# Six local-attention layers: probabilities times tokens instead of times values, Wv and Wo multiplied by head, the FFN's shift made by transfers, and new instruction orders

## The reference, cut to what matters

```python
def shift_tokens(t):                       # the second half of the features comes from the token before
    a, s = jnp.split(t, 2, -1)
    s = jnp.pad(s, ((0, 0), (1, 0), (0, 0)))[:, :-1]
    return jnp.concatenate([a, s], -1)

def attn_layer(x, Wqkv, qs, ksc, Wo):
    q, k, v = heads(jnp.split(x @ Wqkv, 3, -1))
    q, k = l2norm(q) * qs, l2norm(k) * ksc
    ...                                    # q and k are rotated by tables of cosines and sines
    sim = einsum('bhwie,bhwje->bhwij', q, look(k)) * 8; attn = softmax(masked sim)
    out = einsum('bhwij,bhwje->bhwie', attn, look(v))
    return concat_heads(out) @ Wo

def ffn_layer(x, g, bln, W1, b1, W2, b2):
    xn = layernorm(x) * g + bln
    a, gate = jnp.split(xn @ W1 + b1, 2, -1)
    return a * gelu(gate) @ W2 + b2

x = x + relative_attention(layernorm(x))
y = layernorm(x)
for i in range(6):
    y = attn_layer(shift_tokens(y), ...) + y
    y = ffn_layer(shift_tokens(y), ...) + y
return x + y
```

## Time and profile before

| | us |
|---|---|
| median of 3 runs | 2132.15 (2129.59 to 2133.04) |
| the profiled execution | 2129.15 |
| its span | 2127.4 |
| PE busy | 2025.2 (95%) |
| PEld busy | 1357.7 (64%) |
| DVE busy | 1498.2 (70%) |
| ACT busy | 1285.3 (60%) |
| POOL busy | 1521.0 (71%) |
| share of PE in the chain that ended last | 72% |

### The profile page before, as it was taken

How to read it: one execution, slowest core, us unless ns; L and a number is a source line. 1 busy time by engine, 2 the same in 40 slices (tenths; PEclk the granted TensorE clock), 3 DMA queues, 4 the chain that set the end, 5 groups by cost and what they waited for, 6 DMA issues and landing times.

```text
span 2127.4 us, 84221 instructions
## 1 busy us (share of the span) xinstructions
PE 2025.2 (95%) x35763; PEld 1357.7 (64%) x35763; DVE 1498.2 (70%) x2267; ACT 1285.3 (60%) x1844; POOL 1521.0 (71%) x2315
## 2 busy tenths in 40 slices
PE   6899998979999999999999999999999999999997
PEld 2555555545666667766676666766676666766665
DVE  3445454458877788778777788777787788777873
ACT  4676767535655666566655566566665666566653
POOL 4344444468888788777887788778887788877880
PEclk9999999989999999999999999999999999999998
DMA  6999999922224222242232322224222242222221
GB/s 201 331 347 354 340 352 351 328 73 59 65 67 115 63 66 70 62 114 62 63 73 63 111 68 66 63 64 112 67 72 64 61 118 62 67 63 63 66 70 41
DMA packets 121588, 261.51 MB, mean 123 GB/s; under 512 B 29140, under 2 KB 36224, under 8 KB 120448
## 3 DMA queue, kind: packets, MB, share of 16 engines
q1 hardware_dynamic: 121216, 256.13, 41.3%
HBM read 87.06 MB, written 68.29 MB: 73 GB/s over the span
## 4 chain that ended last, share of the span: by engine, by line
PE 72%; POOL 2%; DVE 2%; issue 1%; ACT 1%; POOLq 0%; DVEq 0%; ACTq 0%
PE ring L463 24%; PE ring L529 9%; PE ring L473 8%; PE yps L541 8%; PE ring L499 7%; PE ring L569 5%; PE ring L510 4%; PE tpose L579 3%; PE ring L491 1%; DVE turned L643 1%; PE tpose L551 1%; PE tpose L561 1%; POOL ropes L229 0%; POOL roped L275 0%; PE yps L454 0%
## 5 line engine op out<-in xcount | busy, mean ns | idle before, releaser
L643 DVE TENSOR_TENSOR turned<-ring,ropes 128x1024 f32<-128x1024 f32 x384 | 452.2, 1220 | 301.4 <-PE ring L463 301.4
L240 POOL TENSOR_TENSOR roped<-turned 128x512 f32<-128x512 f32 x384 | 522.1, 1385 | 171.8 <-PE ring L473 171.0
L463 PE MATMUL ring<-wqkv,xT 128*128 128x512 f32 x1152 | 565.2, 614 | 6.1 <-ACT xT L328 4.9
L275 POOL TENSOR_TENSOR roped<-roped,rnorm 128x1024 f32<-128x1024 f32 x192 | 361.2, 1902 | 7.5
L1188 POOL TENSOR_SCALAR less<-less,lowest 128x512 f32<-128x512 f32 x256 | 174.4, 692 | 216.1 <-DVE lowest L1141 216.1
L1141 DVE CUSTOM_DVE_ANT_0 less<-ps_b,shifted 128x512 f32<-128x512 f32 x256 | 166.7, 689 | 211.7 <-issue 89.5
L463 PEld LDWEIGHTS ring<-wqkv,xT 128*128 128x128 f32 x1152 | 197.6, 191 | 161.0 <-issue 149.3
L369 ACT COPY pT<-ring 128x1024 f32<-128x1024 f32 x96 | 97.1, 1012 | 305.3 <-PE ring L510 305.3
L529 PEld LDWEIGHTS ring<-pT,vwin 64*64 64x64 f32 x12288 | 198.3, 134 | 51.4 <-issue 51.1
L317 ACT ACTIVATE squares<-ring 128x1024 f32<-128x1024 f32 x192 | 197.2, 1027 | 55.0 <-DVE turned L643 54.9
L529 PE MATMUL ring<-pT,vwin 64*64 64x32 f32 x12288 | 219.4, 220 | 4.3 <-issue 2.6
(11 more groups left out here) (134 smaller groups left out, 3242.0 us busy)
## 6 DMA issues: line engine op xcount, KB each, us to landing
vwin<-v SPq DMA_DIRECT2D x1536, 64.0 KB, 2.0
shifted<-scratch_w SPq DMA_DIRECT2D x64, 1024.0 KB, 12.0
scratch_w<-wrows SPq DMA_DIRECT2D x48, 1026.0 KB, 10.2
scratch_w<-x SPq DMA_DIRECT2D x16, 1026.0 KB, 9.9
wqkv<-in_l_wqkv SPq DMA_DIRECT2D x6, 1536.0 KB, 6.7
wo<-in_l_wo SPq DMA_DIRECT2D x6, 512.0 KB
w<-in_l_w SPq DMA_DIRECT2D x6, 342.0 KB
w<-in_l_w SPq DMA_DIRECT2D x6, 171.0 KB
```

The costliest lines, as they stand in the source:

```text
L240: nc.gpsimd.tensor_tensor(halves[2][:, :, side, :], halves[0][:, :, side, :], halves[1][:, :, 1 - side, :], ALU.add).then_inc(s[name + "_a ...
L275: nc.gpsimd.tensor_tensor(whole, whole, norm, ALU.mult).then_inc(s[name + "_roped"], 1)
L463: last = nc.tensor.matmul(out[:, half, :], xT[:, t % SEQT * P:(t % SEQT + 1) * P], wqkv[:, layer_of(t), at + half * 512:at + (half + 1) * ...
L643: ins = nc.vector.tensor_tensor(turned[:, n, part, :].rearrange("p (h d) -> p h d", d=DH), heads, table, ALU.mult)
```

## The change

1. **Attention output.** V is no longer made, copied or laid out. TensorE multiplies, for each window of 32 tokens, the tokens themselves (`xwin`, 32 rows x 128 features, for the window and the one before) with the turned probabilities of all 16 heads (512 columns): 8 products of 32 rows a tile in place of 64 small ones. The four windows lie on four groups of 32 rows and write four different banks. ScalarE copies the result in two halves (`xpT`). `project_out` then takes 16 products of 128x128 (one a head, with `wvo`) in place of 8 with `wo`.
2. **Wv Wo.** Once a layer TensorE transposes Wv (8 transposes) and multiplies it by head with Wo (16 products of 64 rows, both row halves of the array in use), ScalarE copies the three results. It is placed at the tiles 10, 11 and 12 of the layer before; for the first layer, ahead of the first tile.
3. **Turned probabilities.** VectorE's own transpose of 32x32 blocks writes `pT` from `probs`; TensorE's 8 transposes and ScalarE's copy go.
4. **Windows and shift by transfers.** `xwin` is filled by 7 transfers a group from `x`, in place of 64. The FFN's shift is two transfers a group into `xs` in SBUF, in place of two products; the statistics and the norm read it there.
5. **First attention.** Its output projection, residual and norm for sequences 0 to 2 are made inside the rounds (`FINISH`, rounds 85, 93 and 101 and the few after each); sequence 3 stays at the start of the layers, and its norm is made in period 8. The input stays in SBUF in `x1` and isn't loaded a second time; the bias is added in rounds 16, 32, 48 and 64. Wqkv of the first layer is loaded at the end of the rounds.
6. **Orders.** The loop of every engine is in a new order, with a longer pipeline: the FFN of a group is spread over periods n-8 to n-12 and its hidden layer over two of them, and `ROOM` is new.

```diff
         @block.tensor
...
+            def attend(t):
+                if live(t):
+                    p = t // SEQT % 2
+                    pe.wait_ge(s["p_turned"], t + 1)
+                    pe.wait_ge(windows_in[p], WINDOWS * (t // SEQT // 2 + 1))
+                    take("O0", t)
+                    take("O1", t)
+                    for half in (1, 0):
+                        for win in range(WT):
+                            rows = slice(W * win, W * win + W)
+                            last = nc.tensor.matmul(pair("O" + str(win // 2))[:, win % 2, :], xwin[rows, p, t % SEQT, half, :],
+                                                    pT[rows, t % 2, :, half, :], start=half == 1, stop=half == 0)
+                    last.then_inc(s["o_made"], 1)
+            def project_out(t):
...
+                    for h in range(HEADS):
+                        last = nc.tensor.matmul(out[:, 0:D], xpT[:, t % 2, h, :, :].rearrange("p w q -> p (w q)"),
+                                                wvo[:, layer_of(t), h // PAIRS, h % PAIRS, :], start=h == 0,
+                                                stop=h == HEADS - 1)
+            def make_wvo(layer, a):
...
+                    for j in range(PAIRS // 2):
+                        for r in range(2):
+                            rows, at = slice(r * DH, (r + 1) * DH), a * PAIRS // 2 + j
+                            last = nc.tensor.matmul(out[:, r, j * D:(j + 1) * D], wvT[rows, at, :], wo[layer % 2][rows, at, :],
+                                                    start=True, stop=True)
         @block.scalar
...
+            def copy_o(t, half):
...
+                    act.wait_ge(s["o_made"], t + 1)
+                    at_least(act, s["y_made"], t - 1)
+                    nc.scalar.copy(xpT[:, t % 2, :, 2 * half:2 * half + 2, :].rearrange("p h w q -> p w h q"),
+                                   pair("O" + str(half)).rearrange("p w (h q) -> p w h q", q=W)
         @block.vector
...
+            def turn_p(t):
+                    dve.wait_ge(s["p_normed"], t + 1)
+                    at_least(dve, s["o_made"], t - 1)
+                    nc.vector.transpose(pT[:, t % 2, :, :, :].rearrange("p h s q -> p (h s q)"),
+                                        probs[:, t % 2, :, :, :].rearrange("p r j k -> p (r j k)")).then_inc(s["p_turned"], 1)
         @block.sync
...
+            def shift(g):
...
+                    sp.wait_ge(s["y_added"], SEQT * (g + 1))
+                    at_least(sp, s["xn_made"], g)
+                    sp.dma_start(xs[1:P, :, :], tiles[0:P - 1, :, :]).then_inc(s["shifted"], 16)
+                    sp.dma_start(xs[0:1, 1:SEQT, :], tiles[P - 1:P, 0:SEQT - 1, :]).then_inc(s["shifted"], 16)
         @block.gpsimd
...
             for n in PERIODS:
-                norms(n - 2)
-                scale(0, n - 2)
-                scale(1, n - 2)
-                add(0, n - 1)
-                add(1, n - 1)
+                add(1, n - 1)
+                add(0, n - 1)
+                deviations(group_of(n - 9))
+                norms(n - 1)
+                scale(1, n - 1)
+                scale(0, n - 1)
+                add_b2(group_of(n - 9))
...
+            FINISH = {85: 0, 93: 1, 101: 2}
...
+                        if c in FINISH:
+                            b = FINISH[c]
+                            pe.wait_ge(s["o_done"], max(turned_units, VARS * (b + 1)))
+                            for i in range(STEPS):
+                                last = nc.tensor.transpose(ps[:, 7, i * P:(i + 1) * P], attn[:, b * STEPS + i, :], ident[:, :])
+                            last.then_inc(s["a_turned"], 1)
```

More of the change, by code:

```diff
@@ L35 @@
 NEWTON = 3
[L36 removed]
+TABLES = 2 * 2 * WT + 4
 def at_least(eng, sem, count):
@@ L379, in copy_xn, with copy_next_wvo @@
+            def copy_next_wvo(t):
+                step, layer = t % (SEQT * BATCH), t // (SEQT * BATCH) + 1
+                if t >= TURN_WV - SEQT * BATCH:
+                    if step == TURN_WV:
+                        copy_wv(layer)
+                    for a in range(2):
+                        if step == TURN_WV + 1 + a:
+                            copy_wvo(layer, a)
             def copy_xn(g):
@@ L432, in _, with take @@
             holder = {}
-            def view(kind, c=0):
-                return bank(kind) if kind in ONE else ring[:, room(kind, c), :, :]
-            def take(kind, at, c=0):
-                r = room(kind, c)
+            def take(kind, at):
+                r = ROOM[kind]
                 if r in holder:
@@ L503, in scores @@
                         last.then_inc(s["scored"], 1)
-            def turn_p(t):
+            def attend(t):
                 if live(t):
-                    pe.wait_ge(s["p_normed"], t + 1)
-                    out = take("PT", t).rearrange("p b c -> p (b c)")
-                    for j in range(PAIRS):
-                        last = nc.tensor.transpose(out[:, j * P:(j + 1) * P],
-                                                   probs[:, t % 2, j, :, :].rearrange("p r k -> p (r k)"), ident[:, :])
-                    last.then_inc(s["p_turned"], 1)
@@ new lines, in project_out, with turn_wv @@
+                    last.then_inc(s["y_made"], 1)
+            def turn_wv(layer):
+                if layer < DEPTH:
+                    layer_in(pe, layer)
+                    out = take("WV", layer).rearrange("p b c -> p (b c)")
+                    for j in range(PAIRS):
+                        at = 2 * INNER + j * P
+                        last = nc.tensor.transpose(out[:, j * P:(j + 1) * P], wqkv[layer % 2][:, at:at + P], ident[:, :])
+                    last.then_inc(s["wv_turned"], 1)
@@ new lines, in make_wvo @@
+            def make_wvo(layer, a):
+                if layer < DEPTH:
+                    pe.wait_ge(s["wvT_copied"], layer + 1)
+                    pe.wait_ge(s["weights"], LOADS * (layer + 1))
+                    out = take("M" + str(a), layer)
+                    for j in range(PAIRS // 2):
+                        for r in range(2):
+                            rows, at = slice(r * DH, (r + 1) * DH), a * PAIRS // 2 + j
+                            last = nc.tensor.matmul(out[:, r, j * D:(j + 1) * D], wvT[rows, at, :], wo[layer % 2][rows, at, :],
+                                                    start=True, stop=True)
+                    last.then_inc(s["wvo_made" + str(a)], 1)
@@ L556, in turn_xn, with next_wvo @@
+            def next_wvo(t):
+                step, layer = t % (SEQT * BATCH), t // (SEQT * BATCH) + 1
+                if t >= TURN_WV - SEQT * BATCH:
+                    if step == TURN_WV:
+                        turn_wv(layer)
+                    for a in range(2):
+                        if step == TURN_WV + 1 + a:
+                            make_wvo(layer, a)
             def turn_xn(g):
@@ L868, in relative_attention @@
             FIRST_KEPT = scratch.shape[0] - 2 * KEPT
[L869 to L870 removed]
+            wrows = sb2("wrows", [P, NW, 2, 2, S + 1])
+            wrows_of = [wrows[:, n, :, :, :] for n in range(NW)]
             shifted = sb2("shifted", [P, NR, 2, 2, S])
@@ L907, in relative_attention, with finished @@
             TURNS = {4: 1, 6: 2, 8: 3}
+            FINISH = {85: 0, 93: 1, 101: 2}
+            def finished(c):
+                return sum(at < c for at in FINISH)
             PROJECTIONS = {0: ("k", 0), 2: ("v", 0)}
@@ L1074, in _ @@
                             last.then_inc(s["o_summed"], 1)
+                        if c in FINISH:
[4 more added lines that the diff above has]
+                            last.then_inc(s["a_turned"], 1)
+                        if c - 2 in FINISH:
+                            b = FINISH[c - 2]
+                            pe.wait_ge(s["a_copied"], b + 1)
+                            pe.wait_ge(later_loaded, LATER)
+                            for i in range(STEPS):
+                                last = nc.tensor.matmul(ps[:, 7, i * D:(i + 1) * D], oT[:, i * P:(i + 1) * P], kept["wo"][:, :],
+                                                        start=True, stop=True)
+                            last.then_inc(s["a_projected"], 1)
                 @block.vector
```

556 lines of the change are left out of this document (263 added, 293 removed).

## The result

| | before | after |
|---|---|---|
| median of the timed runs, us | 2130.87 (2127.71 to 2133.04, 4 runs) | 2179.85 (2177.92 to 2181.59, 4 runs) |
| ratio, 95% interval | 1 | 1.0228 [1.021, 1.0247] |
| span of the profiled run, us | 2127.4 | 2179.8 |
| rounds: to the last copy of the attention's output | 439.0 | 448.1 |
| from there to the first turned x | 14.1 | 16.1 |

What follows compares the result with a forecast made beforehand. TensorE was taken to bound the layers: -5.49 + 4.12 gave -1.4 us a tile, to 15.6. With rounds, start and drain the sum was -109, so 2022 us, range 2000 to 2050 (8 in 10: 1992 to 2078).

Steps and rivals of the forecast that it cites:

- The step that failed: FFN token shift in the layers: transfers land after at least 2.0 us, perhaps 4, hidden before the statistics.
- the 87 periods: Steady part of the layers with FFN: 1.4 us less a tile, -122 us, taken as -113 after gaps.
- GpSimd: Its work a tile in the layers: 14.8 us of the 15.6 us period, the least room of the engines.
- the first rival: In the layers VectorE and GpSimd become the bound, 16.3 us a tile with lumps, 2074 us in all; chance 0.20.
- Wv Wo: TensorE's transposes and products for the combined weights: 3.7 us a layer, 0.23 a tile.
- Rounds: First attention, with sequence ends made inside it: DMA sets the pace, so +1 us (0 to +9).
- Start: Start of the layers: first product at 455 us where it was at 453.96, +1 us (-4 to +4).
- Drain: After the last tiles, by latency of output product, copies, shift and FFN: +4 us.
- output product: TensorE's output projection in the layers doubles from 8 to 16 products: another 1.79 us a tile.
- the attend: TensorE's new attention product in the layers, two sets on four row groups: 2.1 us a tile for 16 records.
- the transpose of 32x32 blocks: VectorE's turn of the probabilities in the layers: 1.2 us a tile, 2.4 as the upper end.
- row groups apart: In the new attend the row groups don't run together: 2200 us two at a time, 2480 one by one; chance 0.04.

Runs made afterwards that it cites:

- k1: Changed kernel with the shift's transfer of 127 rows made as two, of 112 and 15 rows; ratio 0.9676 to the kernel before.
- k3: Changed kernel with the shift's transfer of 127 rows made as two, of 97 and 30 rows; ratio 0.9965 to the kernel before.
- e5: Changed kernel with the shift's transfer of 127 rows asked for tile by tile, as each tile is finished; ratio 0.9665 to the kernel before.
- f2: e5 with the turned Wv and Wv Wo made in the banks of K, ahead of the turn of q; ratio 0.9616 to the kernel before.
- f4: f2 with output projection, residual and norm of all four sequences after the rounds; ratio 0.9607 to the kernel before.
- h2: f4 with Wv Wo made for the first layer alone, so it computes something else; ratio 0.9555 to the kernel before.
- h1: Changed kernel with the shift's transfers at full width, 512 bytes of each token in place of 256; ratio 1.0752 to the kernel before.
- e2: Changed kernel with the shift back on TensorE, two products and one ScalarE copy into xs; ratio 0.9751 to the kernel before.
- the f kernels: f2, f4, and e5 with only the four sequences' attention ends moved after the rounds; ratios 0.9616, 0.9607 and 0.9687 to the kernel before.

## Why the prediction was wrong

**The step that failed** is this one: "The shift's transfers are asked for at about p + 8.7 and land after at least 2.0, as those of vwin; out of 512 short rows perhaps 4. The statistics stand at p + 12: hidden, up to 0.7 late once in four tiles". In the sum for the 87 periods the term was therefore nothing. They land so that the statistics start 9.3 us after the request, 5.8 late. I took the duration of a 64 KB transfer of 32 rows for one of 127 KB of 127 rows and allowed a factor two for short rows; what decides is the outermost dimension, and k1 against k3 prices it. And I gave this unknown no bound from above, only "at least 2.0" and a "perhaps". The rows had one: 64 KB in 2.0 us, should all of it move on one of 16 engines, is up to 32 us. Then the rest was missed too: what is queued behind the statistics (L753, and through it TensorE's next x), and that the clock is lower in the two projections behind that idle of 4.0 us.

The forecast for the 95 periods was 1578.9 - 115 = 1463.9 us; it was 1603.7. Of the 140 us between them:
- the wait and the clock: 108 (e5 has 1495.9; k1, with 1494.4, gives 109);
- the room of Wv Wo: 12 (e5 to f2);
- the rest, 20. About 5 of it lies in the first 12 tiles, for which the forecast's terms give 7 us less than before (2 and four times 1.3), where k1 has 2 less (163.9 for 165.9). The others are groups of 62.9 us on average, 65.6 with Wv Wo (f2), where 62.5 to 62.8 were forecast. GpSimd, which the forecast had at 14.8 of 15.6 us, is in the chain there: POOL has 21% of f4's, against 2% in the kernel before. It may be what is true of the first rival; no kernel here tells it apart.

```profile
PE 44%; POOL 21%; issue 9%; ACT 2%; DVE 1%; DMA 0%; POOLq 0%; ACTq 0%; DVEq 0%
```

**Wv Wo** was put at 3.7 us a layer; by h2 it takes 2.3 in f4, and with the 2.4 a layer that f2 saves, 4.7 in e5. The work was sized too high, and its wait for the copy of q left out.

**Rounds**: +1 was forecast because "DMA sets the pace", +9.1 came. The three units with an end are 6.6 longer together, and 2.6 came in the first unit, before any of this; h1, with the same rounds, doesn't have these 2.6, so they are a difference between runs. VectorE can't subtract scores while it adds and normalises:

```profile
321.61 0.69 DVE L1199 TENSOR_TENSOR x<-ps_b,x 128x512 f32<-128x512 f32 x1 [1.80 <-PE ps_b L1106]
322.34 0.87 DVE L1202 BATCH_NORM_STATS2 norm_stats<-x 128x6 f32<-128x128 f32 x4
323.24 0.38 DVE L1205 BATCH_NORM_AGGREGATE norm_meanvar<-norm_stats 128x2 f32<-128x6 f32 x4
```

A DMA share of 1.02 didn't mean that an engine could stop for 2 us without loss.

**Start**: +2.0 for +1. The first product, at 453.96 before, comes at 465.0, of which the rounds are 9.1. The other 2.0 are Wv Wo, which waits for wo and for its own copies:

```profile
458.50 1.46 PE L573 MATMUL ring<-early,wvT 64*128 64x128 f32 x16 [2.44 <-DMA early<-in_l_wo]
461.15 2.08 PE L573 MATMUL ring<-early,wvT 64*128 64x128 f32 x16 [1.19 <-ACT wvo L396]
```

**Drain**: +16.5 for +4. Without the wait it is +9 to +11 (e2, e5, k1 and the f kernels). The output product was counted once, but the last three tiles' stand nearly one behind the other on TensorE, 3.6 to 3.8 us each where they took 1.8 to 2.1, which is 5 in all; and the last shift by transfer takes 3.4 us in f4, against 1.5 forecast.

**What held**: the attend at 2.00 (2.1 forecast), the output product at 3.57 (3.58), the transpose of 32x32 blocks at 1.23 (1.2), and, once nothing waits, 62.2 us for the quickest four tiles (62.5). Of the rivals, "row groups apart" is refuted by 2.00, and the first one, VectorE and GpSimd as the bound (2074), as the cause of the loss, by the four kernels that keep their work and lose the wait. The division's mean rose from 1484 to 1686 ns. The Trainium skill's rule on the shared port ("SBUF — State Buffer", Who interferes with whom) would have it so, and it decided nothing.

## What to carry to other kernels

Before work is moved to a transfer, write its access pattern beside the one whose duration you borrow: bytes, row length, and above all the outermost dimension; a shift by one row is 127 rows of 128, and 112 + 15 costs 3.7 us where 127 costs 9.3. Bound an unknown transfer from above by what one DMA engine moves (here 18 GB/s in packets of 256 bytes), and then ask what stands behind its reader in the same engine's queue. A term that is called hidden deserves the same two bounds as one that is paid.

## What the runs showed of the hardware

- SyncE's transfers, SBUF to SBUF, rows of 256 bytes: 4 x 127 rows, statistics 9.3 us after the request; 4 x 112 and 4 x 15, 3.7; 4 x 97 and 4 x 30, 7.8. With 127 or 97 rows 1.2 packets are on their way at a time, with 112 and 15 12.6. At full width, 127 packets of 2 KB: 12.7 for 8.5 from issue to landing.
- A request behind a transfer of 127 (or 97) rows took 6.44 (4.84) us to issue; behind one of 112, 1.19; behind the three rows of one partition, 0.74. With the three rows first, VectorE still waits 6.53 us for the large transfer, 5.81 with them last.
- After 4.0 us in which TensorE had nothing to do, the granted clock of the next 7 us was 0.61 (a mix of 2.4 and 1.2 GHz), and 3.44 us of products took 5.86; after another 4.1 us it was 0.76, and after 2.4 us in k3 1.00.
- Four row groups of 32 rows run together when two such sets follow one another, 2.00 us for 16 records, where two sets that each pay the change of form, 2 x 1.07 by the earlier trace rows, would be 2.14.
